# First tropical pass of a fused GNN, LSTM and FFN kernel: seven candidates per token in place of eight, four from columns 0 to 127 and three from columns 128 to 255

## The chip, the cores and the metric

The kernel runs on one core of one Trainium2 chip. The metric is the device time of one execution in microseconds (us), as the median of several runs. Three runs of the kernel before took 6265.23, 6267.40 and 6268.96 us, so the median is 6267.4 us.

## The reference, cut to what matters

Two layers are computed, each a graph convolution followed by a feed-forward part: in the first layer that part is an LSTM, in the second a "tropical" network. Only the tropical part of the second layer is touched. It runs over 16384 tokens of 256 columns and has 1024 outputs for each token:

```python
x = x + _L1_ffn_ref(_layernorm(x, axis=-1), Wt, bt, ...)

def blk_fn(xx):
    t = jnp.max(xx[:, None, :] + Wt[None, :, :], axis=-1) + bt
    z = t[:, :, None]
    cvx = jnp.max(z * sl_cvx[None] + of_cvx[None], axis=-1)
    ccv = jnp.min(z * sl_ccv[None] + of_ccv[None], axis=-1)
    return s * cvx + (1.0 - s) * ccv
```

The costly line is the first: t[f] is the maximum over all 256 columns d of x[d] + Wt[f, d]. [...]

## The kernel before

The stages run one after the other: first graph layer, LSTM, second graph layer, preparation of the hinges, the tropical stage and the feed-forward stage, `stage_ffn`. Each builds its own block of instructions for the engines, so that a stage begins when the one before has ended on all of them. The tropical stage, `stage_tropical`, has five parts: constants, `tropical_first`, `tropical_plan`, `tropical_slots` once for each half of the columns, and `tropical_general`.

**The idea.** The 256 columns of a token are taken in two halves of 128 (`KD = 2`; half 0 is columns 0 to 127, half 1 is columns 128 to 255). Each column is first lifted by the largest weight of that column, y[d] = x[d] + max over f of Wt[f, d], so that a column with a small y can't be the maximum for any f. The weights, lowered by the same maxima, lie on the chip. The columns with the largest y of a token, its candidates, are evaluated exactly for all 1024 outputs. A test then says of every other column whether it can still matter; the columns of which it can't be ruled out are called open below.

**`tropical_first`** runs over 128 tiles of 128 tokens (`TILES`), and takes `FIRST = 4` candidates of each half, 8 in all (`CANDS`). One tile is one slot of a software pipeline with two buffers. In a slot:

- DVE finds for the next tile the eight largest y of each half and where they are (`best`, `find`: L1845, L1851) and copies the places of the first four of each half into `cand` (`name`, L1857).
- PE spreads the places of four candidates over the partitions (`spread`, L1749), and ACT makes of them four 0/1 matrices of 128 by 128 (`turn_hot`: L1684, L1686). A slot has two such groups (`GRP = 4`, `G = 2`).
- PE multiplies each 0/1 matrix with the weights, which are held as a high and a low part, and so puts the weight column of each token's candidate into PSUM: `fetch`, four matmuls of 512 columns (L1764). There are two PSUM buffers for it (`fetched`, `RING = 2`).
- ACT starts `t_out` from candidate 0 (`begin`, L1712). DVE takes candidates 1 to 7 in with one instruction each (`use`, L1869), which adds the candidate's y and takes the maximum over 1024 outputs. The instruction waits for the one before it, since both write `t_out`.
- The test of the slot's tile is spread over two later slots: ACT takes exponentials of t (L1694) and of the columns left (L1699), PE turns them (`turn_fall`, L1776) and multiplies them with exponentials of the weights (`add_up`, L1786), and DVE compares (`test`, L1878). POOL lays out which columns are taken, what is left and how it is lifted (L1624 to L1662), and ACT counts the columns of each half that are done (`count`, L1719).

The order of PE within a slot is written out by hand in `slot`: spread of group 1, then eight fetches with two parts of `add_up`, two parts of `turn_fall`, the spread of group 0 of the next tile (between fetch 5 and fetch 6) and two more parts of `add_up` (behind fetches 6 and 7) between them. A fetch waits for the 0/1 matrices of its group, and for the use of the candidate two before it, which frees its PSUM buffer.

**`tropical_plan`** sorts, for each half and on each of the 128 partitions, the tokens by their number of open columns. The r-th token of every partition goes into slot r, so that a slot's number of columns is the largest of 128 tokens. Slots fall into classes of 16, 8, 6, 4, 3 and 2 candidates (`CLASSES`); the end of each class is rounded up to an even number, and is at least two slots behind the end of the class before it. Slots of tokens that have nothing open aren't run.

**`tropical_slots`**, run for half 0 and then for half 1, gathers in each slot the rows of left columns and of t by indirect DMA issued on POOL, and takes as many candidates as the class says, with the same fetch (L2192) and use (L2260). The first use of a slot reads `ts_tin`, the others read `ts_tout`.

**`tropical_general`** takes the tokens with more than 16 open columns in a half, all 256 columns of eight partitions a round. It runs one round at the least, and 16 rounds for each slot of such tokens.

Of the kernel before, what the change touches and what calls it, by code (L numbers as in the profile page):

```python
# [9 lines left out]
ALU = mybir.AluOpType  # L10
# [1317 lines left out]
CAND = 8  # L1328
TILES = TOK // P
CLASSES = (16, 8, 6, 4, 3, 2)  # L1330
FIRST = 4
SLOTS = TILES + 20
DENSE_RUN = 8
DENSE_RUNS = P // DENSE_RUN
# [182 lines left out]
def tropical_first(nc, v, xn3_dram, left_dram, t_dram):  # L1517


    RING = 2  # L1520
    CANDS = KD * FIRST
    G = CANDS // GRP
    MORE = CANDS - 1
    with ExitStack() as ctx:
        def sb(name, shape, dt=F32):
# [51 lines left out]
        tested, masked, left_ready = sem("tested"), sem("masked"), sem("left_ready")  # L1577
        first_ready, counted = sem("first_ready"), sem("counted")
        block = ctx.enter_context(nc.Block())

        def tiles(eng, slot, last):

# [36 lines left out]
        @block.gpsimd  # L1619
        def _(pool):  # L1620
            def lift(s, j, rows):

                pool.wait_ge(x_in[j], rows)
                pool.tensor_tensor(y[j][:, :, :].rearrange("p k d -> p (k d)"), x[j][:, :], wmax[:, :], ALU.add)\  # L1624
                    .then_inc(y_ready, 1)

            def leave(s, j):

                pool.wait_ge(tested, s + 2)
                wait_past(pool, left_ready, s)  # L1630
                held(2)
                pool.tensor_scalar(mask[:, :], done[j][:, :, :].rearrange("p k d -> p (k d)"), LOW, None, ALU.mult)\
                    .then_inc(masked, 1)
                pool.wait_ge(left_stored[j], (s - j) * 8 + 16)
                pool.wait_ge(masked, s + 1)
                pool.tensor_tensor(left[j][:, :], mask[:, :], rest[j][:, :, :].rearrange("p k d -> p (k d)"), ALU.add)\
                    .then_inc(left_ready, 1)

            def slot(s, j):
                pool.wait_ge(selected, s + 1)  # L1640
                held(0)
                for k in range(KD):
                    last = pool.tensor_scalar(taken[:, k, :], y[j][:, k, :], top[j][:, k, FIRST:FIRST + 1], LOW,
                                              ALU.is_gt, ALU.mult)
                last.then_inc(taken_ready, 1)
                pool.tensor_scalar(next_best[:, :], top[j][:, 0, FIRST:FIRST + 1], top[j][:, 1, FIRST:FIRST + 1], None, ALU.max)\
                    .then_inc(next_best_ready, 1)
                if not isinstance(s, int) or s > 1:
                    leave(s - 2, j)
                    pool.wait_ge(left_ready, s - 1)  # L1650
                pool.wait_ge(taken_ready, s + 1)
                pool.tensor_tensor(rest[j][:, :, :], taken[:, :, :], y[j][:, :, :], ALU.add).then_inc(rest_ready, 1)
                pool.wait_ge(rest_ready, s + 1)
                lift(s + 2, j, 16 + 16 * (s // 2 + 1) if isinstance(s, int) else (s - j + 4) * 8)
                pool.wait_ge(next_best_ready, s + 1)
                pool.tensor_tensor(shift_t[j][:, :], next_best[:, :], scale[:, 0:1], ALU.mult).then_inc(shift_t_ready, 1)
                pool.tensor_tensor(deepest[:, :], next_best[:, :], scale[:, 2:3], ALU.subtract).then_inc(deepest_ready, 1)
                pool.wait_ge(shift_t_ready, s + 1)
                pool.tensor_tensor(shift_r[j][:, :], shift_t[j][:, :], log_share[:, :], ALU.add).then_inc(shift_r_ready, 1)
                pool.wait_ge(deepest_ready, s + 1)  # L1660
                held(1)
                pool.tensor_scalar(rest_low[j][:, :], rest[j][:, :, :].rearrange("p k d -> p (k d)"), deepest[:, :], None,  # L1662
                                   ALU.max).then_inc(rest_low_ready, 1)

            def held(k):

                pool.tensor_tensor(pool_pause[:, k:k + 1], log_share[0:1, :], log_share[0:1, :], ALU.add)

            def last():
                for j in range(2):  # L1670
                    leave(TILES - 2 + j, j)

            pool.memset(log_share[:, :], math.log(SHARE)).then_inc(share_set, 1)
            pool.wait_ge(share_set, 1)
            for j in range(2):
                lift(j, j, 16)
            tiles(pool, slot, last)

        @block.scalar
        def _(act):  # L1680
            def turn_hot(q, b):

                act.wait_ge(index_ready, q + 1)
                act.activation(dist[b][:, :], index[b][:, :], ACT.Abs, bias=v["p_minus"][:, :]).then_inc(dist_ready, 1)  # L1684
                act.wait_ge(dist_ready, q + 1)
                act.activation(one_hot[b][:, :], dist[b][:, :], ACT.Relu, scale=-1.0, bias=1.0)\  # L1686
                   .then_inc(one_hot_ready, 1)

            def fall_off(s, j):
# [18 lines left out]
            def begin(s, j):  # L1708

                act.wait_ge(fetched_ready, s * CANDS + 1)  # L1710
                wait_past(act, t_stored[j], (s - j) * 8)
                act.activation(t_out[j][:, :], fetched[0][:, :], ACT.Identity, bias=top[j][:, 0, 0:1]).then_inc(first_ready, 1)  # L1712

            def count(s, j):

# [27 lines left out]
        def _(pe):  # L1743
            def spread(s, j, g):

                pe.wait_ge(selected, s + 1)
                for c in range(GRP):
                    one = cand[j][:, g * GRP + c:g * GRP + c + 1].to_broadcast([P, P])
                    mm = pe.matmul(index[g][:, c * P:(c + 1) * P], one, ident_b[:, :], start=True, stop=True)  # L1749
                mm.then_inc(index_ready, 1)  # L1750

            def fetch(s, c):

                g, k = c // GRP, c % GRP // 2
                pe.wait_ge(one_hot_ready, s * G + g + 1)
                if c == 2:
                    pe.wait_ge(first_ready, s + 1)
                elif c < 2:
                    pe.wait_ge(fetched_used, s * MORE + c - 1 + RING)
                else:  # L1760
                    pe.wait_ge(fetched_used, s * MORE + c - 2 + RING)
                for h in range(FFN // CH):
                    for part in range(2):
                        mm = pe.matmul(fetched[c % RING][:, h * CH:(h + 1) * CH],  # L1764
                                       one_hot[g][:, c % GRP * P:(c % GRP + 1) * P],
                                       w_part[part][:, k, h * CH:(h + 1) * CH],
                                       start=(part == 0), stop=(part == 1))
                mm.then_inc(fetched_ready, 1)
# [21 lines left out]
            def slot(s, j):  # L1790
                one_back = not isinstance(s, int) or s > 0
                two_back = not isinstance(s, int) or s > 1
                spread(s, j, 1)
                fetch(s, 0)
                if two_back:
                    add_up(s - 2, j, 2)
                fetch(s, 1)
                if two_back:
                    add_up(s - 2, j, 3)
                fetch(s, 2)  # L1800
                fetch(s, 3)
                if one_back:
                    turn_fall(s - 1, 0)
                fetch(s, 4)
                if one_back:
                    turn_fall(s - 1, 1)
                fetch(s, 5)
                spread(s + 1, 1 - j, 0)
                fetch(s, 6)
                if one_back:  # L1810
                    add_up(s - 1, 1 - j, 0)
                fetch(s, 7)
                if one_back:
                    add_up(s - 1, 1 - j, 1)

# [12 lines left out]
        def _(dve):  # L1828
# [25 lines left out]
            def name(s, j):  # L1854
                wait_past(dve, index_ready, G * (s - 1))
                dve.wait_ge(placed, s + 1)
                dve.tensor_copy(cand[j][:, :].rearrange("p (g k r) -> p k g r", g=G, k=KD),  # L1857
                                place[:, :, 0:FIRST].rearrange("p k (g r) -> p k g r", g=G)).then_inc(selected, 1)

            def use(s, j, c):  # L1860

                column = fetched[c % RING]
                value = top[j][:, c % GRP // 2, 2 * (c // GRP) + c % 2:2 * (c // GRP) + c % 2 + 1]
                dve.wait_ge(fetched_ready, s * CANDS + c + 1)
                if c == 1:
                    dve.wait_ge(first_ready, s + 1)
                else:
                    dve.wait_ge(fetched_used, s * MORE + c - 1 + RING)
                dve.scalar_tensor_tensor(t_out[j][:, :], column[:, :], value, t_out[j][:, :], ALU.add, ALU.max)\  # L1869
                   .then_inc(fetched_used, 1)  # L1870
# [930 lines left out]
```

## Time and profile before

| | us |
|---|---|
| median of three runs | 6267.4 |
| span of the profiled execution, first to last instruction | 6263.1 |
| lowest and highest run | 6265.23, 6268.96 |
| stages ahead of `tropical_first` and its constants | to 2416 |
| `tropical_first` | about 2416 to 3806 |
| `tropical_plan` and the start of the slots | 3806 to 3902 |
| slots of half 0 | 3902 to 4368 |
| change of half and start of half 1 | 4368 to 4402 |
| slots of half 1 | 4402 to 4627 |
| `tropical_general` | 4627 to 4680 |
| `stage_ffn` | 4680 to 6263 |

The span is that of one profiled execution; no total time of its own is recorded for it, and the median of the runs stands 4.3 us above it. The engines are PE (matmul), PEld (PE's weight load), DVE (vector), ACT (scalar), POOL (GpSimd) and SP (sync, which issues DMAs). A busy share over the whole span mixes stages with different limits, so the table is to be read stage by stage.

### The profile page before, as it was taken

The numbers are of one execution on the slowest core, as the hardware profiler recorded it, in microseconds if no ns is written. First come the engines' busy times: TensorE is split into PE (matmuls) and PEld (weight loads), VectorE is DVE, ScalarE is ACT, GpSimd is POOL, SyncE is SP. The second block draws the span as 40 slices with busy tenths as digits, with TensorE's granted clock in tenths as the row PEclk, the third lists the DMA queues.
The fourth block names the chain that finished last, engine by engine and source line by source line (L and its number), as shares of the span: only waits on it lengthen the run. The fifth ranks groups of instructions, "written<-read, shape, count | busy, mean of one in ns | idle before, by whom it ended". The sixth has DMA issues, their size and how long they took to land. (4 is left out here: it accounts for less than half of the span.)

```text
span 6263.1 us, 107632 instructions
## 1 busy us (share of the span) xinstructions
PE 5537.4 (88%) x31674; PEld 3591.0 (57%) x31674; DVE 5015.9 (80%) x9353; ACT 3357.1 (54%) x6537; POOL 1709.9 (27%) x3544
## 2 busy tenths in 40 slices
PE   9998999999888835999999994876758999999999
PEld 6666777777677733666666663543434444444444
DVE  7995444444688886999999997996858999999998
ACT  6664444444444413666666662221217777777777
POOL 3330000000344413656565652257340000000000
PEclk9999999999999977999999996997879999999999
DMA  4441000000444422222222221257352222121221
GB/s 135 136 134 49 0 0 0 0 0 0 128 153 154 152 94 79 72 74 72 74 72 74 72 74 38 79 177 240 115 199 75 68 81 87 61 87 66 79 83 47
DMA packets 359540, 528.55 MB, mean 84 GB/s; under 512 B 28000, under 2 KB 298080, under 8 KB 359424
## 3 DMA queue, kind: packets, MB, share of 16 engines
q1 hardware_dynamic: 323120, 401.16, 19.6%
q0 software_dynamic: 36304, 126.13, 5.9%
q8 instruction: 38, 0.62, 0.0%
q14 instruction: 78, 0.64, 0.0%
HBM read 298.06 MB, written 229.13 MB: 84 GB/s over the span
## 5 line engine op out<-in xcount | busy, mean ns | idle before, releaser
L1764 PE MATMUL t_fetched<-t_wpart,t_onehot 128*128 128x512 f32 x4096 | 1222.4, 420 | 35.6 <-DVE t_tout L1869 15.5
L1869 DVE SCALAR_TENSOR_TENSOR t_tout<-t_fetched,t_top,t_tout 128x1024 f32<-128x1024 f32 x896 | 1149.1, 1283 | 36.3 <-PE t_fetched L1764 5.2
L1764 PEld LDWEIGHTS t_fetched<-t_wpart,t_onehot 128*128 128x128 f32 x4096 | 692.2, 189 | 268.9 <-DVE t_tout L1869 131.3
L2686 DVE SCALAR_TENSOR_TENSOR f_line<-f_hinge,f_vec,f_line 128x1024 f32<-128x1024 f32 x512 | 656.8, 1283 | 59.8 <-ACT f_hinge L2570 30.1
L2192 PE MATMUL ts_fetched<-t_wpart,ts_onehot 128*128 128x512 f32 x1608 | 509.7, 453 | 162.1 <-ACT ts_onehot L2167 66.4
L604 PE MATMUL l_ps<-l_wih,l_x 128*64 128x128 f32 (+1 forms) x6144 | 544.5, 312 | 1.0 <-DVE l_ps L530 1.0
L572 ACT ACTIVATE l_act<-l_ps 128x128 f32<-128x128 f32 x1024 | 253.9, 276 | 526.2 <-PE l_ps L604 526.2
L2620 PE MATMUL f_pso<-f_fused,f_wd 128*128 128x512 f32 x1024 | 463.1, 595 | 29.4 <-DVE f_fused L2673 29.4
L2607 PE MATMUL f_psc<-f_x,f_wc 128*128 128x512 f32 x1024 | 488.8, 600 | 0.0
L604 PE MATMUL l_ps<-l_whh,l_ht 128*64 128x128 f32 (+1 forms) x6144 | 488.2, 308 | 0.0
L2192 PEld LDWEIGHTS ts_fetched<-t_wpart,ts_onehot 128*128 128x128 f32 x1608 | 307.5, 209 | 312.5 <-DVE ts_tout L2260 200.7
L2607 PE MATMUL f_psg<-f_x,f_wg 128*128 128x512 f32 x1024 | 481.9, 593 | 0.0
L604 PEld LDWEIGHTS l_ps<-l_wih,l_x 128*64 128x64 f32 x6144 | 374.5, 137 | 106.3 <-issue 1.8
L535 DVE TENSOR_TENSOR l_c<-l_c,l_act 128x128 f32<-128x128 f32 x256 | 75.8, 296 | 446.0 <-ACT l_act L572 446.0
L2164 ACT ACTIVATE ts_dist<-ts_index,t_pminus 128x256 f32<-128x256 f32 (+2 forms) x140 | 79.5, 568 | 654.0 <-PE ts_index L2183 544.1
L604 PEld LDWEIGHTS l_ps<-l_whh,l_ht 128*64 128x64 f32 x6144 | 379.7, 137 | 73.8
L2570 ACT ACTIVATE f_hinge<-f_pst,f_vec 128x1024 f32<-128x1024 f32 x384 | 398.9, 1114 | 0.0
L2260 DVE SCALAR_TENSOR_TENSOR ts_tout<-ts_fetched,ts_top,ts_tout 128x1024 f32<-128x1024 f32 x296 | 380.0, 1284 | 14.1 <-PE ts_fetched L2192 3.4
L2620 PEld LDWEIGHTS f_pso<-f_fused,f_wd 128*128 128x128 f32 x1024 | 191.9, 190 | 284.6 <-issue 255.9
L2607 PEld LDWEIGHTS f_psg<-f_x,f_wg 128*128 128x128 f32 x1024 | 195.3, 191 | 246.8 <-issue 246.8
L2577 ACT ACTIVATE f_spare<-f_pst,f_vec 128x1024 f32 x224 | 240.7, 1135 | 175.4 <-DVE f_pause L2711 175.4
L2686 DVE SCALAR_TENSOR_TENSOR f_line<-f_spare,f_vec,f_line 128x1024 f32<-128x1024 f32 x224 | 287.8, 1285 | 44.2 <-DVE f_line L2686 44.2
(388 smaller groups left out, 10696.8 us busy)
## 6 DMA issues: line engine op xcount, KB each, us to landing
t<-t_tout SPq DMA_DIRECT2D x128, 512.0 KB, 2.6
f_t<-t SPq DMA_DIRECT2D x64, 1024.0 KB, 5.2
g_adj<-in_adj SPq DMA_DIRECT2D x128, 256.0 KB, 3.0
g_adjt<-in_adjt SPq DMA_DIRECT2D x128, 256.0 KB, 2.7
t_x<-x_normalised SPq DMA_DIRECT2D x130, 128.0 KB, 2.4
g_x<-in_x SPq DMA_DIRECT2D x64, 256.0 KB, 2.8
x_kept<-g_x SPq DMA_DIRECT2D x64, 256.0 KB, 2.2
g_x<-x_kept SPq DMA_DIRECT2D x64, 256.0 KB, 2.8
```

Source lines behind the costliest of these rows:

```text
L572: act.activation(act_g[q][:, :], gate(j, q), function).then_inc(act_ready[q], 1)
L604: mm = pe.matmul(out[:, :, 0:P] if n > 1 else ps_g[j][c2 * HB:(c2 + 1) * HB, q * LANE:q * LANE + P], source[:, k, :], w[:, k, q:q + n, c2, ...
L1764: mm = pe.matmul(fetched[c % RING][:, h * CH:(h + 1) * CH], one_hot[g][:, c % GRP * P:(c % GRP + 1) * P], w_part[part][:, k, h * CH:(h + 1 ...
L1869: dve.scalar_tensor_tensor(t_out[j][:, :], column[:, :], value, t_out[j][:, :], ALU.add, ALU.max)\
L2164: act.activation(dist[b][:, 0:n * P], index[b][:, 0:n * P], ACT.Abs, bias=v["p_minus"][:, :])\
L2192: mm = pe.matmul(fetched[buf][:, h * CH:(h + 1) * CH], one_hot[b][:, at * P:(at + 1) * P], w_part[part][:, half, h * CH:(h + 1) * CH], sta ...
L2260: dve.scalar_tensor_tensor(t_out[j][:, :], column[:, :], top[j][:, c:c + 1], (t_out if c else t_in)[j][:, :], ALU.add, ALU.max).then_inc(f ...
L2570: op = act.activation(hinge[v][:, k, :], ps_t[:, :], ACT.Relu, bias=column(u, "knot", k))
L2577: act.activation(spare[:, ds(k, 1), :].rearrange("p o t -> p (o t)"), ps_t[:, :], ACT.Relu, bias=column(u, "knot", k + SURE))
L2607: mm = pe.matmul(ps_[:, :], w_[:, k, u * P:(u + 1) * P], x[j][:, k, h * HB:(h + 1) * HB], start=(k == 0), stop=(k == KD - 1))
L2620: mm = pe.matmul(ps_o[k][:, h * HB:(h + 1) * HB], w_d[:, u, k * P:(k + 1) * P], fused[u % 2][:, h * HB:(h + 1) * HB], start=(u == 0), stop ...
L2686: dve.scalar_tensor_tensor(acc[:, :], source, column(u, "bend", k), acc[:, :], ALU.mult, ALU.add)\
```

## The change

`FIRST` becomes a pair: four candidates of half 0 and three of half 1. Candidates 0 to 3 are now those of half 0 and candidates 4 to 6 those of half 1 (`which`); before, each group of four held two of each half. The second group is three wide, for PE's spread and for ACT's two activations. Since seven is odd, the PSUM buffer of candidate c is found from the tile's parity too (`ring`). `name` makes two copies, one for each half, in place of one. `slot` on PE loses fetch 7; the spread for the next tile still follows fetch 5, part 0 of `add_up` now stands ahead of the last fetch, and part 1 behind it. Nothing is changed in the plan, the slots, the general part or any other stage, but their loop counts are read from the data that `tropical_first` leaves.

```diff
--- before.py
+++ after.py
@@ -1328,7 +1328,7 @@
 CAND = 8
 TILES = TOK // P
 CLASSES = (16, 8, 6, 4, 3, 2)
-FIRST = 4
+FIRST = (4, 3)
 SLOTS = TILES + 20
 DENSE_RUN = 8
 DENSE_RUNS = P // DENSE_RUN
@@ -1518,8 +1518,9 @@
 
 
     RING = 2
-    CANDS = KD * FIRST
-    G = CANDS // GRP
+    CANDS = sum(FIRST)
+    GROUPS = [min(GRP, CANDS - c) for c in range(0, CANDS, GRP)]
+    G = len(GROUPS)
     MORE = CANDS - 1
     with ExitStack() as ctx:
         def sb(name, shape, dt=F32):
@@ -1578,6 +1579,14 @@
         first_ready, counted = sem("first_ready"), sem("counted")
         block = ctx.enter_context(nc.Block())
 
+        def which(c):
+
+            return (0, c) if c < FIRST[0] else (1, c - FIRST[0])
+
+        def ring(j, c):
+
+            return (j * CANDS + c) % RING
+
         def tiles(eng, slot, last):
 
             for s in range(4):
@@ -1640,10 +1649,11 @@
                 pool.wait_ge(selected, s + 1)
                 held(0)
                 for k in range(KD):
-                    last = pool.tensor_scalar(taken[:, k, :], y[j][:, k, :], top[j][:, k, FIRST:FIRST + 1], LOW,
+                    last = pool.tensor_scalar(taken[:, k, :], y[j][:, k, :], top[j][:, k, FIRST[k]:FIRST[k] + 1], LOW,
                                               ALU.is_gt, ALU.mult)
                 last.then_inc(taken_ready, 1)
-                pool.tensor_scalar(next_best[:, :], top[j][:, 0, FIRST:FIRST + 1], top[j][:, 1, FIRST:FIRST + 1], None, ALU.max)\
+                pool.tensor_scalar(next_best[:, :], top[j][:, 0, FIRST[0]:FIRST[0] + 1], top[j][:, 1, FIRST[1]:FIRST[1] + 1],
+                                   None, ALU.max)\
                     .then_inc(next_best_ready, 1)
                 if not isinstance(s, int) or s > 1:
                     leave(s - 2, j)
@@ -1680,10 +1690,11 @@
         def _(act):
             def turn_hot(q, b):
 
+                hots = slice(0, GROUPS[b] * P)
                 act.wait_ge(index_ready, q + 1)
-                act.activation(dist[b][:, :], index[b][:, :], ACT.Abs, bias=v["p_minus"][:, :]).then_inc(dist_ready, 1)
+                act.activation(dist[b][:, hots], index[b][:, hots], ACT.Abs, bias=v["p_minus"][:, :]).then_inc(dist_ready, 1)
                 act.wait_ge(dist_ready, q + 1)
-                act.activation(one_hot[b][:, :], dist[b][:, :], ACT.Relu, scale=-1.0, bias=1.0)\
+                act.activation(one_hot[b][:, hots], dist[b][:, hots], ACT.Relu, scale=-1.0, bias=1.0)\
                    .then_inc(one_hot_ready, 1)
 
             def fall_off(s, j):
@@ -1709,7 +1720,7 @@
 
                 act.wait_ge(fetched_ready, s * CANDS + 1)
                 wait_past(act, t_stored[j], (s - j) * 8)
-                act.activation(t_out[j][:, :], fetched[0][:, :], ACT.Identity, bias=top[j][:, 0, 0:1]).then_inc(first_ready, 1)
+                act.activation(t_out[j][:, :], fetched[ring(j, 0)][:, :], ACT.Identity, bias=top[j][:, 0, 0:1]).then_inc(first_ready, 1)
 
             def count(s, j):
 
@@ -1744,14 +1755,14 @@
             def spread(s, j, g):
 
                 pe.wait_ge(selected, s + 1)
-                for c in range(GRP):
+                for c in range(GROUPS[g]):
                     one = cand[j][:, g * GRP + c:g * GRP + c + 1].to_broadcast([P, P])
                     mm = pe.matmul(index[g][:, c * P:(c + 1) * P], one, ident_b[:, :], start=True, stop=True)
                 mm.then_inc(index_ready, 1)
 
-            def fetch(s, c):
-
-                g, k = c // GRP, c % GRP // 2
+            def fetch(s, j, c):
+
+                g, k = c // GRP, which(c)[0]
                 pe.wait_ge(one_hot_ready, s * G + g + 1)
                 if c == 2:
                     pe.wait_ge(first_ready, s + 1)
@@ -1761,7 +1772,7 @@
                     pe.wait_ge(fetched_used, s * MORE + c - 2 + RING)
                 for h in range(FFN // CH):
                     for part in range(2):
-                        mm = pe.matmul(fetched[c % RING][:, h * CH:(h + 1) * CH],
+                        mm = pe.matmul(fetched[ring(j, c)][:, h * CH:(h + 1) * CH],
                                        one_hot[g][:, c % GRP * P:(c % GRP + 1) * P],
                                        w_part[part][:, k, h * CH:(h + 1) * CH],
                                        start=(part == 0), stop=(part == 1))
@@ -1791,25 +1802,24 @@
                 one_back = not isinstance(s, int) or s > 0
                 two_back = not isinstance(s, int) or s > 1
                 spread(s, j, 1)
-                fetch(s, 0)
+                fetch(s, j, 0)
                 if two_back:
                     add_up(s - 2, j, 2)
-                fetch(s, 1)
+                fetch(s, j, 1)
                 if two_back:
                     add_up(s - 2, j, 3)
-                fetch(s, 2)
-                fetch(s, 3)
+                fetch(s, j, 2)
+                fetch(s, j, 3)
                 if one_back:
                     turn_fall(s - 1, 0)
-                fetch(s, 4)
+                fetch(s, j, 4)
                 if one_back:
                     turn_fall(s - 1, 1)
-                fetch(s, 5)
+                fetch(s, j, 5)
                 spread(s + 1, 1 - j, 0)
-                fetch(s, 6)
                 if one_back:
                     add_up(s - 1, 1 - j, 0)
-                fetch(s, 7)
+                fetch(s, j, 6)
                 if one_back:
                     add_up(s - 1, 1 - j, 1)
 
@@ -1854,13 +1864,15 @@
             def name(s, j):
                 wait_past(dve, index_ready, G * (s - 1))
                 dve.wait_ge(placed, s + 1)
-                dve.tensor_copy(cand[j][:, :].rearrange("p (g k r) -> p k g r", g=G, k=KD),
-                                place[:, :, 0:FIRST].rearrange("p k (g r) -> p k g r", g=G)).then_inc(selected, 1)
+                for k, at in ((0, 0), (1, FIRST[0])):
+                    last = dve.tensor_copy(cand[j][:, at:at + FIRST[k]], place[:, k, 0:FIRST[k]])
+                last.then_inc(selected, 1)
 
             def use(s, j, c):
 
-                column = fetched[c % RING]
-                value = top[j][:, c % GRP // 2, 2 * (c // GRP) + c % 2:2 * (c // GRP) + c % 2 + 1]
+                column = fetched[ring(j, c)]
+                k, r = which(c)
+                value = top[j][:, k, r:r + 1]
                 dve.wait_ge(fetched_ready, s * CANDS + c + 1)
                 if c == 1:
                     dve.wait_ge(first_ready, s + 1)
```

## Rows read from the trace of the kernel before

**Rows 1.** Stages: engines' busy us (instructions), clock, DMA share, GB/s.

```profile
2422.00:3794.00 1372.00, 1337.58 (x7089) 862.20 (x7088) 1317.28 (x2149) 882.43 (x1512) 820.06 (x1764) 1.00 0.20 72
...
4524.00:4627.00 103.00, 70.08 (x235) 42.09 (x233) 80.89 (x188) 20.49 (x46) 84.65 (x167) 0.83 0.74 255
4627.00:4680.00 53.00, 21.20 (x64) 13.88 (x64) 21.89 (x21) 0.00 (x0) 6.56 (x11) 0.66 0.17 58
```

**Rows 2.** Tile t_tout: count, duration in ns, first and last start.

```profile
L1869 DVE SCALAR_TENSOR_TENSOR t_tout<-t_fetched,t_top,t_tout x896: 1271/1284/1287, 2422.3 to 3803.7; 128x1024 f32<-128x1024 f32 x180
L1712 ACT ACTIVATE t_tout<-t_fetched,t_top x128: 1114/1117/1120, 2420.6 to 3794.2; 128x1024 f32<-128x1024 f32 x128
```

**Rows 3.** Waits, 2500 to 3700 us: total us, times, longest.

```profile
POOL t_poolpause L1667 <- DVE t_done L1878: 440.7, 111, 4.1
...
PEld t_fetched L1764 <- DVE t_tout L1869: 118.1, 334, 0.7
```

**Rows 4.** Timeline of one slot of the first pass: start, us, instruction.

```profile
3008.32 0.16 DVE L1857 CAST t_cand<-t_place 128x8 bf16<-128x8 uint32 x1
3008.44 1.28 DVE L1869 SCALAR_TENSOR_TENSOR t_tout<-t_fetched,t_top,t_tout 128x1024 f32<-128x1024 f32 x1
...
3009.97 6.59 DVE L1869 SCALAR_TENSOR_TENSOR t_tout<-t_fetched,t_top,t_tout 128x1024 f32<-128x1024 f32 x5
...
3011.30 1.20 PE L1764 MATMUL t_fetched<-t_wpart,t_onehot 128*128 128x512 f32 x4
...
3012.34 0.40 PE L1749 MATMUL t_index<-t_identb,t_cand 128*128 128x128 bf16 x4
3012.62 1.20 PE L1764 MATMUL t_fetched<-t_wpart,t_onehot 128*128 128x512 f32 x4
...
3013.50 0.63 ACT L1686 ACTIVATE t_onehot<-t_dist 128x512 fp32r<-128x512 f32 x1
...
3015.00 0.39 PE L1786 MATMUL t_pssum<-t_expw,t_fallt 128*128 128x256 bf16 x2
3015.23 0.39 PE L1749 MATMUL t_index<-t_identb,t_cand 128*128 128x128 bf16 x4
3015.43 1.19 PE L1764 MATMUL t_fetched<-t_wpart,t_onehot 128*128 128x512 f32 x4
...
3016.65 1.11 ACT L1712 ACTIVATE t_tout<-t_fetched,t_top 128x1024 f32<-128x1024 f32 x1 [2.52 <-PE t_fetched L1764]
...
3017.87 1.28 DVE L1869 SCALAR_TENSOR_TENSOR t_tout<-t_fetched,t_top,t_tout 128x1024 f32<-128x1024 f32 x1
```

**Rows 5.** Timeline: two small copies of DVE, one behind the other.

```profile
4644.70 0.15 DVE L2366 COPY tg_fromnow<-t_densefrom 128x1 int32 x1
4644.76 0.14 DVE L2367 COPY tg_tonow<-t_denseto 128x1 int32 x1
```

**Rows 6.** Half 0: count of slots, and first slots of classes 4 and 2.

```profile
L2260 DVE SCALAR_TENSOR_TENSOR ts_tout<-ts_fetched,ts_top,ts_tin x70: 1282/1284/1285, 3901.9 to 4365.8; 128x1024 f32<-128x1024 f32 x70
...
4107.45 1.28 DVE L2260 SCALAR_TENSOR_TENSOR ts_tout<-ts_fetched,ts_top,ts_tin 128x1024 f32<-128x1024 f32 x1 [0.16 <-issue]
...
4210.43 1.28 DVE L2260 SCALAR_TENSOR_TENSOR ts_tout<-ts_fetched,ts_top,ts_tin 128x1024 f32<-128x1024 f32 x1 [0.16 <-issue]
```

**Rows 7.** Half 1: count, first slots of classes 16, 8, 3, 2, last slot.

```profile
L2260 DVE SCALAR_TENSOR_TENSOR ts_tout<-ts_fetched,ts_top,ts_tin x36: 1283/1284/1285, 4402.5 to 4624.3; 128x1024 f32<-128x1024 f32 x36
...
4402.47 1.28 DVE L2260 SCALAR_TENSOR_TENSOR ts_tout<-ts_fetched,ts_top,ts_tin 128x1024 f32<-128x1024 f32 x1 [0.55 <-PE ts_fetched L2192]
...
4448.85 1.28 DVE L2260 SCALAR_TENSOR_TENSOR ts_tout<-ts_fetched,ts_top,ts_tin 128x1024 f32<-128x1024 f32 x1 [0.16 <-issue]
...
4503.29 1.28 DVE L2260 SCALAR_TENSOR_TENSOR ts_tout<-ts_fetched,ts_top,ts_tin 128x1024 f32<-128x1024 f32 x1 [0.16 <-issue]
...
4524.48 1.28 DVE L2260 SCALAR_TENSOR_TENSOR ts_tout<-ts_fetched,ts_top,ts_tin 128x1024 f32<-128x1024 f32 x1 [0.15 <-issue]
...
4624.29 1.28 DVE L2260 SCALAR_TENSOR_TENSOR ts_tout<-ts_fetched,ts_top,ts_tin 128x1024 f32<-128x1024 f32 x1 [0.43 <-DMA t<-ts_tout,ts_now]
```

## The prediction, made before the changed kernel was run

> **What bounds the kernel now.** I read the stages first, since no stage overlaps the next: a change inside the tropical stage is worth what that stage gets shorter or longer. In the first pass DVE is busy 1317 of 1372 us (96%) and PE 1338 (97%), at a granted clock of 1.00, which is the 2.4 GHz level [rows 1]. Both can't be the limit, and PE's busy time is a modelled one, so I went on to the tile that both meet at. The first and the last start on ACT stand 1373.6 us apart for 127 steps [rows 2]: a slot takes 10.816 us. Seven uses of 1.284 us [rows 2] are 9.0 us of it, and they come no closer than 1.33 us apart: five of them last 6.59 us from the first start to the last end [rows 4], that is (6.59 - 1.28) / 4 = 1.327. The waits say which engine is ahead. PE's weight load waits for the uses of DVE in 334 fetches of the window, 118 us in all [rows 3], and no wait of DVE for a fetch is in that view. So DVE sets the pace, with PE close behind: a fetch issued at 3011.30 is followed by the next PE instruction at 3012.34 [rows 4], so it holds PE for 1.04 us, and eight of them are 8.3 of the 10.8 us. POOL idles 440.7 us over 111 slots behind the test [rows 3], 4.0 us a slot, and is no limit.
>
> Then I read what the first pass leaves. Half 0 has 70 slots, half 1 has 36 [rows 6, 7]. In the classes of 2 candidates the slot is not set by the uses: POOL is busy 84.65 of 103 us, with three indirect DMAs a slot, and DVE 80.89 [rows 1].
>
> **The change, part by part: the first pass.** Removed in each slot are one use (1.327 us of DVE's chain) and one fetch (1.04 us of PE). Added or moved are three things.
>
> The second copy in `name`. It stands between use 1 and use 2. The first copy starts at 3008.32, and use 2 starts at 3008.44, as soon as use 1 (started 1.327 before) allows [rows 4]: one copy is hidden in the hand-over between the uses. Two small copies in a row start 0.06 us apart [rows 5]. The bounds are 0 (the second fits in as well) and its whole length, 0.16; I take 0.06, by the nearest row. The skill has a rule that speaks against this edit. The Trainium skill, VectorE: DVE Perf Modes, section on the TRN2 errata, says that every DVE instruction pays a fixed latency of about 150 cycles however small it is, which at its 0.96 GHz is 0.16 us. The copy's length of 0.16 us agrees with it, the spacing of rows 5 does not, and by the rule the gain below would be estimated 13 us smaller.
>
> PE's new order at the end of the slot. Let U3 be the end of use 3, at 11.25 in the row of five [rows 4]. Fetch 5 starts 0.05 behind it, the spread follows at +1.09. Before, fetch 6 came next and waited for use 4 in any case: it started at 3012.62, 1.37 behind U3. Now the spread (0.20, from 3015.23 to 3015.43) and then two matmuls of `add_up` (0.17 to 0.23, from 3015.00 to 3015.23 at most) stand ahead of the last fetch [rows 4], which so starts 1.09 + 0.20 + 0.20 = 1.49 behind U3, 0.12 late. A fetch takes 1.22 us from its start to its reader's (3015.43 to 3016.65 [rows 4]), so that the last use would start at 2.71 to 2.76 behind U3 where the chain of uses has it at 2.69: 0.05 late. No row has this order; the bounds are 0 and 0.19 (all of 0.25 with a slack of 0.06).
>
> Fetch 0 of the next tile. It was 1.13 ahead of the end of the last use. Now it stands behind the last fetch (1.04), `add_up` (0.20) and a spread (0.20), at 1.49 + 1.44 = 2.93 behind U3, while the last use ends at 4.02: 1.09 ahead at best. Its 0/1 matrices have lost one fetch of cover: the spread at 12.34 gave them at 3013.50 + 0.63 = 14.13, 1.79 later, now 1.09 + 1.79 = 2.88 behind U3, with a hand-over just at the same 2.93 [rows 4]. ACT's `begin` and use 1 follow it in a fixed row (3016.65 to 3017.87, 1.22 us), and it was 0.08 us behind DVE's own search already. I take 0.08 for what slips here, between 0.04 and 0.30 (the matrices late, clock or hand-over off).
>
> Sum for a slot: 1.327 - 0.06 - 0.05 - 0.08 = 1.137, I round to 1.13; bounds 1.28 and 0.83 (not all at their worst at once: 1.327 - 0.10 - 0.12 - 0.28). Over 127 steps it is 143 us, between 105 and 162. ACT's narrower group and POOL lie under DVE and cost or give nothing: POOL keeps 4.0 - 1.1 = 2.9 us of slack.
>
> **What is given back: the slots of half 1.** The fourth column of half 1 is no longer taken. Where it can't be ruled out, it is one more open column, so a token's count goes from n to n + 1, and tokens with none open get a slot. I read the present slots as a ladder: the number of slots in which the column of rank r is still open. Half 0: rank 5, 70 slots; rank 7, 34 (those before the first of class 2); rank 9, 16 (before the first of class 4), counted as first uses between these rows [rows 6]. Half 1: rank 5, 36; rank 7, 12 (before 4524.48); rank 8, at most 8 (before 4503.29) [rows 7]. As shares of 128 on the scale of a normal distribution half 0 stands at +0.12, -0.63 and -1.15, that is 0.37 a rank and then 0.26: the steps grow by 1.44 in two ranks towards the top. Half 1 stands at -0.58 and -1.32, 0.37 a rank; one and a half ranks further up the step is some 0.48, and rank 4 comes to -0.10, a share of 0.46, 59 slots. I take 58. Read by half 0's ladder alone (the rung above 34 lies at about 50) it is 50; with a step of 0.6 it is 66. Rank 6 by the same steps gives 20 to 24, I take 22.
>
> The price of a slot: class 16, (4448.85 - 4402.47) / 2 = 23.2 us; classes 8, 6 and 4, two slots each, 54.4 us together, which is 1.32 a candidate and 1.14 a slot: 11.7, 9.1, 6.4; class 3, 5.2 (5.3 in the rows, with one wait in it); class 2, (4624.29 - 4524.48) / 23 = 4.34 [rows 7]. Half 1 now is 2, 2, 2, 2, 4 and 24 slots of classes 16, 8, 6, 4, 3 and 2: 226 us. With ends at 2, 4, 8, 12, 22 and 58 it is 46.4 + 23.4 + 36.4 + 25.6 + 52 + 36 x 4.34 = 340 us, 114 more. With 50 slots and ends at 2, 4, 6, 12, 20 it is 72 more; with 66 and 24 it is 150 more, and if the two deepest classes each end a pair later, 178.
>
> Half 0 is touched too: t is the maximum of seven candidates, so lower in a few outputs, and the test a little easier to fail. One pair of class 2 costs 8.7 us; I take 4, between 0 and 17.
>
> **The sum.** 6263.1 - 143 + 114 + 4 = 6238 us of span. With the same 4.3 us around it, the median is 6242 us, 0.4% faster. Measured medians of this kernel differ by about 0.2% (12.5 us) without a change, so this is about twice what can be told from nothing.
>
> **The rivals.**
>
> *The fourth column is seldom open (15%).* Half 0's ladder speaks for it. Growth 72 in place of 114 (and the first pass as above): 6196 us.
>
> *The slots give it all back (19%).* One mechanism: more tokens of half 1 get a slot than the ladder says. The point from which it decides is a growth of 139 us, about 64 slots in half 1 with the other ends as taken. At 66 slots, with one pair in half 0, it is -143 + 150 + 9, 6283 us; with the deeper classes a pair longer, 6311. For it: the steps of the ladder grow towards the top, and a slot is as wide as the worst of its 128 tokens, so that few tokens make a slot. Against: the step would have to be 0.6, more than any seen.
>
> *PE takes DVE's place (12%).* The last fetch and fetch 0 come 0.25 and 0.3 us late in every slot, since PE must now do spread, `add_up` and fetch in a row; the slot takes 9.98 us. Gain 105: 6283 us with the growth as taken. Against it: PE's work adds up to 7 x 1.04 + 0.8 (`add_up`) + 0.5 (`turn_fall`) + 0.4 (spreads) = 9.0 us, less than the slot.
>
> *A token comes to 17 open columns (4%).* `tropical_general` runs its one round now, in a stage of 53 us [rows 1], so no token has 17. A single one with 16 in half 1 would make 32 rounds of it; a round has sixteen steps of 1.3 us and some gathers, about 28 us, and 31 more are 870: 7110 us. Half 1's ladder is thinner than half 0's at each rung, and half 0 has none either, so it is unlikely.
>
> That the change does nothing is excluded: a candidate less is a use less in each of 128 slots.
>
> **How the numbers follow.** The forecast has 50%, its own range 6215 to 6262. Chances: faster by over 0.2%, the forecast nearly whole and the first rival, 63%; within 0.2%, 17%, from the second and third rival's near side; slower, 20%, their far side and the fourth. The range reaches from 6192 (the first rival with a slightly better first pass) to 6288 (the second and third), and leaves the deeper classes and the general part outside.
>
> **What the changed profile would show.** L1869 x768, its starts on ACT 9.6 to 9.8 us apart; DVE above 95% busy still, and no DVE wait for a fetch beyond 0.2 us. The last fetch's start 1.4 to 1.5 us behind the end of use 3. Copies at L1857's place x258. Half 0's first uses x70 or x72, half 1's x56 to x60. The general part with one round. The prediction is wrong in size if half 1 has 50 or 66 slots, and wrong in kind if PE idles less and DVE waits in each slot.

## The result, and the profile after

The changed kernel takes 7258.2 us (7255.9 to 7260.2, four runs) against 6268.1 us before (four runs): a ratio of 1.158, 95% interval [1.157, 1.159]. It is 990 us slower, where 0.4% faster was forecast, and far outside the range. The fourth rival happened, the one that was given 4%: the general part runs 32 rounds in place of one.

Read in the order of the prediction, every stage but that one is near its forecast. The tile `t_tout` of the changed kernel (count, duration in ns, first and last start; its lines are 11 and 12 further down) answers to [rows 2]:

```profile
L1881 DVE SCALAR_TENSOR_TENSOR t_tout<-t_fetched,t_top,t_tout x768: 1272/1283/1286, 2421.2 to 3654.3; 128x1024 f32<-128x1024 f32 x192
L1723 ACT ACTIVATE t_tout<-t_fetched,t_top x128: 1113/1117/1121, 2419.5 to 3646.1; 128x1024 f32<-128x1024 f32 x128
```

A slot takes (3646.1 - 2419.5) / 127 = 9.658 us, where 9.69 was forecast. The first uses of the slots of half 0, and below them those of half 1, answer to the counts of [rows 6, 7]:

```profile
L2272 DVE SCALAR_TENSOR_TENSOR ts_tout<-ts_fetched,ts_top,ts_tin x70: 1282/1283/1286, 3752.6 to 4224.1; 128x1024 f32<-128x1024 f32 x70
...
L2272 DVE SCALAR_TENSOR_TENSOR ts_tout<-ts_fetched,ts_top,ts_tin x52: 1282/1283/1285, 4260.9 to 4570.1; 128x1024 f32<-128x1024 f32 x52
```

Half 0 keeps 70 slots, but in classes of 4, 4, 8, 8, 12 and 34 where it had 4, 2, 10, 8, 10 and 36 (for 16, 8, 6, 4, 3 and 2 candidates). Half 1 has 52 in classes of 2, 2, 4, 4, 8 and 32; 58 were forecast, 50 to 66 the bounds. The general part's copy that opens each of its rounds:

```profile
L2376 DVE CAST tg_runrows<-t_ident x32: 693/694/696, 4584.9 to 5625.7; 128x1024 fp32r x32
```

A round takes (5625.7 - 4584.9) / 31 = 33.6 us. The busy view of the stages (PE, PEld, DVE, ACT, POOL, clock, DMA share, GB/s) shows in its second row that no engine is the limit in the general part: DVE has 702 of 1083 us, and PE's granted clock is 0.76, so that part of the stage is spent at the 1.2 GHz level.

```profile
2420.00:3655.00 1235.00, 1208.73 (x6504) 780.56 (x6503) 1167.10 (x2166) 862.97 (x1525) 825.45 (x1776) 1.00 0.23 81
...
4583.00:5666.00 1083.00, 680.57 (x2048) 455.23 (x2048) 702.21 (x672) 0.00 (x0) 110.77 (x193) 0.76 0.11 35
```

The timeline between two rounds says why a round is more than its 21 us of uses:

```profile
4985.23 1.22 DVE L2397 TENSOR_TENSOR tg_tout<-tg_acc 128x1024 f32<-128x1024 f32 x1
...
4986.87 1.00 POOL L2338 DMA_INDIRECT t<-tg_tout,tg_tonow  x1 [0.16 <-issue]
4990.30 0.18 POOL L2329 TENSOR_TENSOR tg_poolpause<-tg_poolzero 1x1 f32<-1x1 f32 x1 [2.43 <-DMA t<-tg_tout,tg_tonow]
4990.70 0.69 DVE L2376 CAST tg_runrows<-t_ident 128x1024 fp32r x1 [4.25 <-POOL tg_poolpause L2329]
...
4997.65 0.43 DVE L2381 TENSOR_TENSOR tg_y<-tg_x,t_wmax 128x256 f32<-128x256 f32 x1 [6.14 <-DMA tg_tin<-t,tg_fromnow]
4998.40 1.28 DVE L2393 SCALAR_TENSOR_TENSOR tg_acc<-tg_fetched,tg_y,tg_tin 128x1024 f32<-128x1024 f32 x1 [0.32 <-DVE tg_y L2381]
```

DVE stands still for 4.25 us until the store of the round has landed, and for 6.14 us until the next round's gathers have: no round overlaps another.

The span grew by 991.0 us, and it adds up from the first instructions of the stages:

| stretch, first start to first start | before | after | difference |
|---|---|---|---|
| start to `begin` of tile 0 | 2420.6 | 2419.5 | -1.1 |
| first pass, 127 slots | 1373.6 | 1226.6 | -147.0 |
| plan, to the first use of half 0 | 107.7 | 106.5 | -1.2 |
| half 0, to the first use of half 1 | 500.6 | 508.3 | +7.7 |
| half 1, to the end of its last use | 224.4 | 311.8 | +87.4 |
| general part, to the first load of the last stage | 50.4 | 1093.8 | +1043.4 |
| last stage | 1585.9 | 1587.6 | +1.7 |

### The profile page after: what moved, and what is told of

Read it like the earlier page. It is cut to its first block and busy times, and to the rows that moved or that the text cites. A ratio compares the mean times of both kernels' runs of the same rounds, so it can differ in the third digit from the quotient of the medians.

```text
span 7254.1 us, 113957 instructions
## 1 busy us (share of the span) xinstructions
PE 6127.0 (84%) x33288; PEld 3988.6 (55%) x33288; DVE 5617.0 (77%) x10155; ACT 3347.3 (46%) x6573; POOL 1874.9 (26%) x3842
## 5 line engine op out<-in xcount | busy, mean ns | idle before, releaser
L1775 PE MATMUL t_fetched<-t_wpart,t_onehot 128*128 128x512 f32 x3584 | 1064.5, 419 | 27.2 <-DVE t_tout L1881 1.7
L1881 DVE SCALAR_TENSOR_TENSOR t_tout<-t_fetched,t_top,t_tout 128x1024 f32<-128x1024 f32 x768 | 984.5, 1282 | 48.2 <-PE t_fetched L1775 4.9
L2359 PE MATMUL tg_fetched<-t_wpart,tg_runrows 128*128 128x512 f32 x2048 | 680.6, 484 | 400.4 <-DVE tg_runrows L2376 258.9
L2359 PEld LDWEIGHTS tg_fetched<-t_wpart,tg_runrows 128*128 128x128 f32 x2048 | 455.2, 236 | 625.6 <-issue 272.5
L1775 PEld LDWEIGHTS t_fetched<-t_wpart,t_onehot 128*128 128x128 f32 x3584 | 606.0, 189 | 244.3 <-DVE t_tout L1881 99.1
L2204 PE MATMUL ts_fetched<-t_wpart,ts_onehot 128*128 128x512 f32 x1824 | 575.2, 451 | 183.3 <-ACT ts_onehot L2179 69.3
L2393 DVE SCALAR_TENSOR_TENSOR tg_acc<-tg_fetched,tg_y,tg_acc 128x1024 f32<-128x1024 f32 x448 | 546.7, 1277 | 31.4 <-PE tg_fetched L2359 29.9
L2204 PEld LDWEIGHTS ts_fetched<-t_wpart,ts_onehot 128*128 128x128 f32 x1824 | 347.4, 208 | 352.5 <-DVE ts_tout L2272 215.0
L2272 DVE SCALAR_TENSOR_TENSOR ts_tout<-ts_fetched,ts_top,ts_tout 128x1024 f32<-128x1024 f32 x334 | 428.8, 1284 | 13.0 <-PE ts_fetched L2204 0.8
```

What stands on the lines that cost most here:

```text
L1775: mm = pe.matmul(fetched[ring(j, c)][:, h * CH:(h + 1) * CH], one_hot[g][:, c % GRP * P:(c % GRP + 1) * P], w_part[part][:, k, h * CH:(h + ...
L2204: mm = pe.matmul(fetched[buf][:, h * CH:(h + 1) * CH], one_hot[b][:, at * P:(at + 1) * P], w_part[part][:, half, h * CH:(h + 1) * CH], sta ...
L2272: dve.scalar_tensor_tensor(t_out[j][:, :], column[:, :], top[j][:, c:c + 1], (t_out if c else t_in)[j][:, :], ALU.add, ALU.max).then_inc(f ...
L2359: mm = pe.matmul(fetched[buf][:, h * CH:(h + 1) * CH], one_row, w_part[part][:, k, h * CH:(h + 1) * CH], start=(part == 0), stop=(part == 1))
L2393: op = dve.scalar_tensor_tensor(acc[c % 2][:, :], row[:, :], value, (t_in if c == 0 else acc[c % 2])[:, :], ALU.add, ALU.max)
```

## The experiments

Kernels that were run together share the runs of the kernel before; those had medians of 6263.6, 6263.2 and 6266.1 us in the three groups. With the 6268.1 us of the result they lie within 0.1% of each other, where the prediction took 0.2%. A kernel that is given without a ratio ran once; it is read by its counts and by the times of its stages, not by its total.

**One round only.** Is the general part all of the loss?

```diff
-then(dve.tensor_scalar(dense[:, 1:2], dense[:, 1:2], 1.0, None, ALU.max))
+then(dve.tensor_scalar(dense[:, 1:2], dense[:, 1:2], 1.0, 1.0, ALU.max, ALU.min))
```

> The changed kernel with the general part held to one round, so that the columns beyond the sixteenth of the deepest tokens are left out. Theory (the whole slowdown is 31 more rounds of the general part at 33.6 us): 7254 - 31 x 33.6, a span of 6213 us, some 50 us under the kernel before, with the first pass at 9.66 us a slot and 52 slots of half 1 as in the changed kernel. Rival (the rounds hide something that costs elsewhere, in the feed-forward stage or at the change of stage): a span well over 6230 us, up to no gain.

Measured: 6207.1 us, ratio 0.991 [0.989, 0.993]; the span is 6205.7, 7 us under the 6213 expected. The 31 rounds are the whole slowdown, and without them the change would be 0.9% faster, more than was forecast. The rival falls.

**Which half.** The count of rounds is taken from half 0 alone.

```diff
-then(dve.tensor_scalar(dense[:, 1:2], even[:, K, 1:2], even[:, K, 0:1], float(DENSE_RUNS), ALU.add, ALU.mult))
+then(dve.tensor_scalar(dense[:, 1:2], even[:, K, 0:1], float(DENSE_RUNS), None, ALU.mult))
```

> The changed kernel with the rounds of the general part counted from half 0 alone; if the deep token is in half 1 its columns beyond the sixteenth are left out. Theory A (the token with 17 open columns is in half 1, where the fourth column is no longer taken): 1 round, a span of 6213 us. Theory B (half 0 had a token with 16 and t, the maximum of seven, is lower now, so that a 17th can't be ruled out): 32 rounds, a span of 7254 us.

Measured: 7247.9 us, a span of 7246.1, and the opening copy of a round 32 times:

```profile
L2376 DVE CAST tg_runrows<-t_ident x32: 693/694/695, 4581.8 to 5618.6; 128x1024 fp32r x32
```

Theory B holds: the deep token is in half 0, whose four candidates were not touched. The prediction had looked for it in half 1.

**What changed for half 0.** Two things reach it: t is the maximum of seven candidates, and the common shift of the exponentials comes from another column. The first experiment keeps eight candidates in t and only leaves the fourth column of half 1 to the test.

```diff
# kernel before
-top[j][:, k, FIRST:FIRST + 1], LOW,
+top[j][:, k, FIRST - k:FIRST - k + 1], LOW,
```

> The kernel before, all eight candidates in t, but the fourth column of half 1 is not marked as taken, so that the test judges it. Theory (in half 0 the new open columns come from t, which is the maximum of seven and so lower): half 0 as before, 4, 2, 10, 8, 10, 36 slots of classes 16, 8, 6, 4, 3, 2, and one round of the general part; half 1 grows to at most the 52 slots of the changed kernel, since only its own column is judged anew and t is higher: 48 to 52; the first pass at 10.82 us a slot; a span of 6263 + 65 to 88 us, 6328 to 6351. Rival (the growth of half 1 is itself mostly from the lower t): half 1 near its 36 slots.

Measured: 6346.5 us, a span of 6344.7. Half 0 is that of the kernel before in every class, and half 1 that of the changed kernel in every class (2, 2, 4, 4, 8, 32); the general part has one round. Its first uses, half 0 and then half 1:

```profile
L2260 DVE SCALAR_TENSOR_TENSOR ts_tout<-ts_fetched,ts_top,ts_tin x70: 1283/1284/1286, 3898.4 to 4363.6; 128x1024 f32<-128x1024 f32 x70
...
L2260 DVE SCALAR_TENSOR_TENSOR ts_tout<-ts_fetched,ts_top,ts_tin x52: 1283/1284/1285, 4400.2 to 4710.0; 128x1024 f32<-128x1024 f32 x52
```

So the two effects come apart. That the fourth column is no longer taken costs half 1 its 16 slots and changes no class of half 0. What happened to half 0 has another cause.

The second experiment is the changed kernel with the old shift.

```diff
-pool.tensor_scalar(next_best[:, :], top[j][:, 0, FIRST[0]:FIRST[0] + 1], top[j][:, 1, FIRST[1]:FIRST[1] + 1],
+pool.tensor_scalar(next_best[:, :], top[j][:, 0, FIRST[0]:FIRST[0] + 1], top[j][:, 1, FIRST[0]:FIRST[0] + 1],
```

> The changed kernel with the exponentials' common shift taken from the fifth column of half 1 as before, in place of the fourth; t and the columns taken are those of the changed kernel. Theory (half 0's 17th column comes from the lower t): 32 rounds, 70 and 52 slots in the same classes, a span of 7250 us. Rival (the new shift rounds the exponentials otherwise and moves borderline columns): one round, half 0 with 2 slots of class 8 and 10 of class 6 as before, a span of about 6205 us.

Measured: 7254.0 us, a span of 7252.2, the classes of both halves as in the changed kernel, and 32 rounds:

```profile
L2376 DVE CAST tg_runrows<-t_ident x32: 693/694/696, 4584.9 to 5623.7; 128x1024 fp32r x32
```

The shift is not it. And the two experiments differ from each other, in what the test gets, in t alone: both leave the fourth column of half 1 to the test, both take the shift from the fifth columns, and t is the maximum of eight candidates in the first and of seven in the second. That one difference takes half 0 from classes of 4, 2, 10, 8, 10 and 36 to 4, 4, 8, 8, 12 and 34, and the general part from one round to 32. So the lower t is the cause.

**How deep the token is.** The deepest class takes 18 candidates in place of 16, with a third search of eight behind the two in its slots; the plan then sends only tokens with more than 18 to the general part.

```diff
-CLASSES = (16, 8, 6, 4, 3, 2)
+CLASSES = (18, 8, 6, 4, 3, 2)
...
-    ROUNDS = 2
-    STEPS = 4
+    ROUNDS = 3
+    STEPS = 2 * ROUNDS
...
+for r in range(rounds):
+    eight = slice(r * CAND, r * CAND + CAND)
+    dve.max(top[j][:, eight], src[:, :]).then_inc(select_steps, 1)
...
+        dve.match_replace(y_left[r][:, :], top[j][:, eight], src[:, :], LOWEST).then_inc(select_steps, 1)
```

> The changed kernel with 18 candidates in the deepest class in place of 16, and a third search of eight in its slots. Theory (the deepest token has 17 or 18 open columns in a half): the general part is back to one round; each of the four slots of half 0 and two of half 1 in the class costs 2 x 1.32 + 1.0 us more, 20 us in all, so a span of about 6235 us, 0.45% under the kernel before. Rival (the deepest token has 19 or more): 32 rounds stay, a span of about 7275 us.

Measured: 6227.4 us, ratio 0.994 [0.993, 0.996], one round. The deepest token has 17 or 18 open columns, and the wider class costs 20.3 us over the kernel held to one round, as worked out.

**The second copy.** The kernel before, with its copy of the places cut in two.

```diff
-dve.tensor_copy(cand[j][:, :].rearrange("p (g k r) -> p k g r", g=G, k=KD),
-                place[:, :, 0:FIRST].rearrange("p k (g r) -> p k g r", g=G)).then_inc(selected, 1)
+for k in range(KD):
+    last = dve.tensor_copy(cand[j][:, :].rearrange("p (g k r) -> p k g r", g=G, k=KD)[:, k],
+                           place[:, :, 0:FIRST].rearrange("p k (g r) -> p k g r", g=G)[:, k])
+last.then_inc(selected, 1)
```

> The kernel before with the copy of the candidates' places made as two copies, nothing else. Theory (a second small copy is mostly hidden in the hand-over between two uses): start to start in the first pass 10.82 to 10.88 us for 10.816, 0 to 8 us in all. Rival (each vector instruction pays its whole 0.16 us): 10.98 us, 20 us in all.

Measured: 6266.7 us; the starts of `begin` run from 2419.5 to 3793.4, which is 10.818 us a slot for 10.816. The second copy costs nothing that can be seen, the lower of the two bounds. One slot's timeline shows where it stands; use 1 started at 3006.15 and ran to 3007.43:

```profile
3007.35 0.23 DVE L1858 CAST t_cand<-t_place 128x4 bf16<-128x4 uint32 x2
3007.48 1.28 DVE L1871 SCALAR_TENSOR_TENSOR t_tout<-t_fetched,t_top,t_tout 128x1024 f32<-128x1024 f32 x1
```

Both copies have started before use 2 does, 1.33 us behind the start of use 1, which is the pace of the uses: the second is hidden in the hand-over like the first.

**PE's order.** On top of the class of 18, the spread for the next tile goes ahead of fetch 5.

```diff
                 if one_back:
                     turn_fall(s - 1, 1)
+                spread(s + 1, 1 - j, 0)
                 fetch(s, j, 5)
-                spread(s + 1, 1 - j, 0)
                 if one_back:
                     add_up(s - 1, 1 - j, 0)
                 fetch(s, j, 6)
```

> The kernel with the class of 18 (median 6227 us, 9.66 us a slot), with PE's spread for the next tile ahead of fetch 5 in place of behind it. Theory (what the first pass lacks against one use less, 0.17 us a slot, is the last fetch 0.07 late and fetch 0 of the next tile late, both for want of room behind fetch 5): start to start 9.50 to 9.56 us, 13 to 20 us less, a median of 6207 to 6215 us. Rival (fetch 5, now behind a turn and a spread, 0.48 us, comes late itself and DVE waits there): 9.66 us or more, 6227 us or more.

Measured: 6208.3 us, ratio 0.991 [0.990, 0.993], 19 us under the class of 18 alone. The two timelines, first that of the changed kernel and then that with the early spread, show where it was:

```profile
3014.60 1.19 PE L1775 MATMUL t_fetched<-t_wpart,t_onehot 128*128 128x512 f32 x4
...
3016.01 1.19 PE L1775 MATMUL t_fetched<-t_wpart,t_onehot 128*128 128x512 f32 x4
...
3017.56 1.20 PE L1775 MATMUL t_fetched<-t_wpart,t_onehot 128*128 128x512 f32 x4
```

```profile
3011.18 1.19 PE L1775 MATMUL t_fetched<-t_wpart,t_onehot 128*128 128x512 f32 x4
...
3012.50 1.20 PE L1775 MATMUL t_fetched<-t_wpart,t_onehot 128*128 128x512 f32 x4
...
3013.91 1.18 PE L1775 MATMUL t_fetched<-t_wpart,t_onehot 128*128 128x512 f32 x4
```

These are fetches 5, 6 and, of the next tile, 0. The last fetch follows fetch 5 after 1.41 us in the changed kernel and after 1.32 with the early spread, which is just the pace of the uses; fetch 0 follows after 2.96 and 2.73. The slot shrinks to 9.472 us, a little below the 9.50 to 9.56 expected:

```profile
L1723 ACT ACTIVATE t_tout<-t_fetched,t_top x128: 1114/1117/1121, 2417.7 to 3620.7; 128x1024 f32<-128x1024 f32 x128
```

**The mirror.** Does the ladder of slots carry over? Three candidates of half 0, four of half 1.

```diff
-FIRST = (4, 3)
+FIRST = (3, 4)
```

> The change mirrored: three candidates of half 0 and four of half 1, the deepest class 16. Theory (the ladder of slots says what a fourth column not taken costs): half 0's rung for rank 4 is 86 to 98 slots, with about 10 slots down to class 8, 24 down to 6, 34 down to 4, 50 down to 3: some 160 us more than before; half 1 36 to 38 slots; the first pass at 9.66 us a slot; the token of half 0 with 16 open columns has 17, so 32 rounds, a span of 7300 to 7350 us. Rival (the ladder doesn't carry over): fewer than 80 slots of half 0.

Measured: 7334.3 us, a span of 7332.5, 32 rounds, 88 slots of half 0 (6, 6, 12, 12, 14, 38) and 38 of half 1. The ladder holds, at the low end of the 86 to 98 that it gave, as for half 1 in the changed kernel (52 for 50 to 66). From the first use of half 0 to the first of half 1 it is 4418.0 - 3753.3 = 664.7 us for 500.6, 164 us more. Half 1 was the better half to take three from, by 78 us (spans of 7332.5 and 7254.1).

**Twice the price by rounding.** The slots for the general part are counted without rounding up to an even number.

```diff
-dense = sb("dense", [1, 2])
+dense, exact = sb("dense", [1, 2]), sb("exact", [1, KD])
...
+dve.tensor_copy(exact[:, :], ps_most[:, KD * K:KD * K + KD])
...
-dve.tensor_copy(dense[:, 0:1], even[:, K, 0:1])
-then(dve.tensor_scalar(dense[:, 1:2], even[:, K, 1:2], even[:, K, 0:1], float(DENSE_RUNS), ALU.add, ALU.mult))
+dve.tensor_copy(dense[:, 0:1], exact[:, 0:1])
+then(dve.tensor_scalar(dense[:, 1:2], exact[:, 1:2], exact[:, 0:1], float(DENSE_RUNS), ALU.add, ALU.mult))
```

> The changed kernel (class 16) with the number of slots for the general part not rounded up to an even one. Theory (one slot holds all tokens that need it, and the rounding doubles the price): 16 rounds of 33.6 us, a span of 7254 - 537 = 6717 us. Rival (two slots are needed): 32 rounds, 7254 us.

Measured: 6710.4 us, 16 rounds. One slot holds every token that needs it; the other 16 rounds were run for an empty slot. How many of its 128 tokens need it, no run shows.

**The version that beats both.** The early spread with a deepest class of 17; the cut below is against the kernel with the class of 18 and the early spread.

```diff
-CLASSES = (18, 8, 6, 4, 3, 2)
+CLASSES = (17, 8, 6, 4, 3, 2)
```

> The kernel with the class of 18 and the early spread (median 6208 us), with the deepest class at 17. Theory (the deepest token has 17 open columns, one more than the kernel before leaves it): one round of the general part, and one use (1.32 us) less in each of six slots, 8 us: a median of 6200 us, 1.0% under the kernel before. Rival (it has 18): 32 rounds, about 7240 us.

Measured: 6201.1 us, ratio 0.990 [0.988, 0.991], 1.0% faster than the kernel before, and one round:

```profile
L2374 DVE CAST tg_runrows<-t_ident x1: 695/695/695, 4579.1 to 4579.1; 128x1024 fp32r x1
```

So the deepest token has exactly 17 open columns: one more than the class of 16 holds. That one column more, in one slot of half 0, costs the 1040 us that turn the gain into a loss of 990.

## Why the prediction was wrong

**The first pass was right in its size and in where it loses time.** 1.13 us a slot was forecast and 1.158 measured, 147 us for 143. Part of the nearness is luck: the delays of PE were taken a little too small, at 0.13 us together for some 0.17, and the second copy at 0.06 too large, and the two errors offset. Of the three terms taken off the use, the last fetch's delay (0.05) is there: the last four uses take 5.33 us from the first start to the last end in the changed kernel where three steps of 1.327 and one use are 5.26, 0.07 more. What slips at fetch 0 was taken at 0.08: from the end of the last use to use 1 of the next tile it was 1.31 us (3009.97 + 6.59 to 3017.87 [rows 4]) and is 1.44 in the slot below.

```profile
3013.28 5.33 DVE L1881 SCALAR_TENSOR_TENSOR t_tout<-t_fetched,t_top,t_tout 128x1024 f32<-128x1024 f32 x4
...
3020.05 1.28 DVE L1881 SCALAR_TENSOR_TENSOR t_tout<-t_fetched,t_top,t_tout 128x1024 f32<-128x1024 f32 x1
```

That slot is above the mean: over the slots of tiles 10 to 117 the same stretch takes 1.34 us on average before and 1.43 after, so 0.09. The two together, 0.07 and 0.09, are nearly all of the 0.17 us that a mean slot lacks against one use less (10.816 - 1.327 = 9.489 for 9.658), and moving the spread gave all of it back. The second copy, taken at 0.06, measured 0.00. The Trainium skill, VectorE: DVE Perf Modes, section on the TRN2 errata, gives a fixed latency of about 150 cycles for each instruction; an estimate from it puts the second copy at 0.16 us a slot, 20 us over the pass. The run with two copies does not agree: its slot is longer by 0.002 us. PE did not take DVE's place: each of the two fetches came late by a tenth of a us at most, on average.

**The growth of half 1 was the right mechanism, somewhat too large.** 114 us was forecast and 87 measured, 52 slots for 58. The term that was off is the ladder's step towards the top, made to grow as half 0's does (0.48 a rank): with half 1's own 0.37 it would have been 53 slots. The mirror lies low in its range in the same way. The experiment on the fourth column gives half 1 the same 52 slots in the same classes with t as before, so nothing else is in its count of slots.

**Half 0 was right as a sum and wrong as a thought.** 4 us were taken and 7.7 measured. But the reasoning, "so lower in a few outputs, and the test a little easier to fail", was turned into pairs of the shallowest class, and it acts all along the ladder: two slots went from class 6 to class 8, two from class 2 to class 3, and the deepest token from at most 16 open columns to 17.

**The step that failed is the last rival's, and with it the general part, which the sum puts at nothing and which grew by 1043 us.** "A single one with 16 in half 1 would make 32 rounds of it": it was looked for only in the half whose candidate was taken away. The sentence that made it unlikely, "half 0 has none either", was true of 17 columns and says nothing of 16. A slot of class 16 shows only that some token has between 9 and 16, so no row of the profile excluded a token one column short of the edge, which a slightly lower t could push over. The ladder does not settle it either: its rungs count slots, each as wide as the worst of its 128 tokens, and its deepest rung is rank 9, eleven ranks short of the sixteenth open column. So the 4% had no row behind it, and half 0, whose ladder is the thicker one at each rung, was given no chance at all, although the prediction itself had said that its t is lower. The size of a round was off too, 33.6 for 28 us, since the one round of before had no store of a round before it to wait for: most of the difference is the 4.25 us of that wait. Two small slips stand in the rivals' working: the 6196 us of the first is a span, without the 4.3 us that the others have, and the third adds up to 6280 us and not 6283. Neither changes the forecast.

What stays open: how many tokens came to 17 open columns in the one slot of half 0, and where 7 us come from by which holding the general part to one round took off more than 31 rounds of 33.6 us (7254.1 - 6205.7 = 1048 us of span for 1042).

## What to carry to other kernels

Where a kernel's work depends on its data, look for thresholds before pricing the smooth part: this change was worth 147 us of gain and 95 us of growth, both forecast within 30 us, and was decided by one slot of tokens, the deepest of which came to 17 open columns where 16 were provided for. A trace shows the class that a case fell into, not how far it stood from the edge, so a path that costs 33.6 us a round and comes 32 rounds at a time deserves its own chance, worked out for everything that the change can move, not only for the part that it edits. When one instruction is taken from a pipeline whose two engines are both above 95% busy, write out the order of the second engine again: here one moved spread was worth 19 us.

## What the runs showed of the hardware

Two small copies between dependent vector instructions were free, 10.818 us a slot for 10.816. The wait for the instruction before them covers both, although each is recorded with about 0.16 us: in the run with two copies they start 1.20 us and more behind the start of use 1, while it still runs, and use 2 starts at the same pace of 1.33 us as elsewhere.
